# A flag's sense reversed: which of two bodies stands first in TensorE's program

## The chip, the core and the metric

The kernel runs on one core of one Trainium2 chip. The metric is the device time of one execution in microseconds (us). Five engines work side by side, each on its own instruction stream: TensorE (PE in the profile; its weight loads are PEld), VectorE (DVE), ScalarE (ACT), GpSimd (POOL) and SyncE (SP). They meet only through semaphores.

## The reference

Two transformer-like blocks on x of 8 sequences x 512 tokens x 128 features. Layer 0 adds a state-space branch and then a feed-forward branch; layer 1 adds a gated linear attention and a feed-forward of LoRA experts. What matters here is the feed-forward of layer 0:

```
_tlin(x, w, s) = einsum('bsi,oi->bso', x, w) * s
h = silu(_tlin(x, w1_w, w1_s)) * _tlin(x, w2_w, w2_s)
h = gelu(_tlin(h, h1_w, h1_s))
h = gelu(_tlin(h, h2_w, h2_s))
return _tlin(h, w3_w, w3_s)
```

The weights w1_w to w3_w are ternary: -1, 0 or 1, in float32.

## The kernel before

The program has two stages. `front` computes the modulations, the state-space branch and the feed-forward of layer 0 for all eight sequences; `attention_lora` computes layer 1. Each stage is one block in which every engine has a hand-written stream, and ends with two barriers of all engines, one at the block's end (shown at L445 for the first stage) and one behind the clearing of the semaphores (L148).

Activations of the feed-forward are split into two rounded parts, high and low (`h_hi`, `h_lo`, `ffn_g_hi`, `ffn_g_lo`), so that two fast products of type float32r with rounded weights `w_hi` give the result of float32. This is right only if the weights are exact in the rounded type. ACT sums the low halves of all weights (L819, `w_junk`), PE adds the four sums (L1063), DVE turns the result into a flag of one number (L641, `w_inexact`), and PE reads the flag into a register (L1172) and branches (L1173). If it is set, PE runs `run(False, ...)`, whose products take the raw weights as plain float32; if not, `run(True, ...)`, whose products take `w_hi` as float32r. With the reference's ternary weights the flag is 0 and `run(True, ...)` runs. Both bodies do the same work in the same order: the transposition of the first normalised sequence (`flip_ffn`, whose instructions have L243), the first tiles (L1113 for the high part, L1117 for the low part), then four pairs of sequences with 24 tiles each (L1072, L1073), and in the end the transposition of the last two results (`flip_y`, again L243). They signal the same semaphores as often, so the other engines' streams don't know which one ran.

In the program of PE the `If` body comes first and the `Else` body behind it. The `If` body ends with a jump over the `Else` body to the stage's end; the `Else` body is followed by the stage's end. PE's part ahead of the branch is `prepare`.

Around the branch the other engines do this. DVE: flag (L641), moments of sequence 0 (`moments_ffn`: L483, L487, L492), modulations (L526), moments of `z` of sequence 1, `apply_ffn(0)` which writes `h_full` (L513), `centre(1)` (L563), `update_centred(1)` (L571), `moments_ffn(1)`, `low_h(0)` which writes `h_lo` (L586), `apply_ffn(1)` (L513). GpSimd: the reciprocal roots (L713) and the addition of a bias to x (L726). ACT: `bring_ffn(0)`, which writes `h_hi` and then `ffn_h` from the transposition (L249). At the stage's end ACT scales the last result (`bring_y`, L836), PE transposes it, and DVE adds it to x (L590).

Of the kernel before, what the change touches and what calls it, by code (L numbers as in the profile page):

```python
# [18 lines left out]
I32 = mybir.dt.int32  # L19
I16 = mybir.dt.int16  # L20
ACT = mybir.ActivationFunctionType
ALU = mybir.AluOpType
# [48 lines left out]
def build(nc, d, out):  # L71

    with ExitStack() as ctx:
        def sb(name, shape, dt=F32):
            return ctx.enter_context(nc.sbuf_tensor(name, shape, dt))

        r = {"set_up": ctx.enter_context(nc.semaphore("set_up"))}

        r["x"] = sb("x", [P, B, T, D])
        r["cols"] = sb("cols", [P, COLS])  # L80
        r["ident"] = r["cols"][:, C_IDENT:C_IDENT + P]
        r["neg_half"] = sb("neg_half", [P, T])
        r["mod"] = sb("mod", [P, 2, 4, B])
        r["gain_ffn0"] = sb("gain_ffn0", [P, B])
        r["l1"] = sb("l1", [P, L1COLS])
        r["wo"] = r["l1"][:, L_WO:L_WO + 2 * D].rearrange("p (q n) -> p q n", q=2)
        r["ar1"] = r["l1"][:, L_AR1:L_AR1 + AR]
        r["war2"] = r["l1"][:, L_WAR2:L_BG].rearrange("p (k n) -> p k n", k=KH)
        r["low_rows"] = r["l1"][:, L_LOW:L_LOW + 1]
        r["gate_bias"] = sb("gate_bias", [P, 1])  # L90
        r["eye8"] = sb("eye8", [P, NH])
        r["ones"] = sb("ones", [P, P])


        with ExitStack() as layer0:
            def sb0(name, shape):
                return layer0.enter_context(nc.sbuf_tensor(name, shape, F32))

            r["gain_attn0"], r["bias_attn0"] = sb0("gain_attn0", [P, B, D]), sb0("bias_attn0", [P, B, D])
            r["ssm_u"] = sb0("ssm_u", [2 * SD, S])  # L100
            for name, shape in (("out", [P, T, D]), ("hT", [P, S]), ("state", [P, S]), ("zn", [P, T, D])):
                r[f"ssm_{name}"] = [sb0(f"ssm_{name}{s}", shape) for s in range(2)]

        r["v_hi"] = sb("v_hi", [P, VCOLS], F32R)
        r["v_lo"] = sb("v_lo", [P, VCOLS], F32R)
        r["m_hi"] = sb("m_hi", [P, NH, P], F32R)
        r["m_lo"] = sb("m_lo", [P, NH, P], F32R)
        r["sel"] = sb("sel", [P, NH, P], F32R)
        r["sel32"] = sb("sel32", [P, 2, P], F32R)
        r["b1s"] = sb("b1s", [3 * GLO, HID], F32R)  # L110
        r["b2s"] = sb("b2s", [3 * GLO, D], F32R)
        r["gain_attn1"] = sb("gain_attn1", [P, B, D])
        r["gain_ffn1"] = sb("gain_ffn1", [P, B, D])
        r["h_split"] = [[sb(f"h_{q}{s}", [P, S], F32R) for q in ("hi", "lo")] for s in range(2)]
        r["h_full"] = [sb(f"h_full{s}", [P, S]) for s in range(2)]
        r["norm_out"] = [sb(f"norm_out{s}", [P, S]) for s in range(2)]
        psum = [ctx.enter_context(nc.psum_tensor(f"bank{n}", [P, S], F32)) for n in range(8)]

        with ExitStack() as block0:
            def sb0(name, shape, dt=F32):  # L120
                return block0.enter_context(nc.sbuf_tensor(name, shape, dt))

            r["w_hi"] = sb0("w_hi", [P, WCOLS], F32R)
            r["w_raw"] = sb0("w_raw", [P, WCOLS])
            r["w_inexact"] = sb0("w_inexact", [1, 1], I32)
            r["w_scale"] = r["cols"][:, C_SCALE:C_SCALE + 4 * KH].rearrange("p (k m) -> p k m", k=4)
            r["wp"] = r["cols"][:, C_WP:C_WP + SD]
            front(nc, d, r, psum)
        attention_lora(nc, r, psum, out)
# [123 lines left out]
def front(nc, d, r, psum):  # L253
# [17 lines left out]
    with ExitStack() as ctx:  # L271
# [62 lines left out]
        w_high, w_summed, w_flagged = sem("w_high"), sem("w_summed"), sem("w_flagged")  # L334
# [70 lines left out]
        def full_at(*use):  # L405

            return AT[use] + 1

        def bank(*use):
            return psum[HOME[use]]  # L410
# [34 lines left out]
        with nc.Block() as block:  # L445
# [32 lines left out]
            def _(dve):  # L478
# [15 lines left out]
                def moments_in(b):  # L494
                    dve.wait_ge(loaded_x[b if b < SLOTS else 1 + b // 2], 16)
                    moments(n_in, b, lambda t: x_of(b)[:, t, :])

                def moments_out(b):
                    dve.wait_ge(mm, full_at("z", b))
                    moments(n_out, b, lambda t: bank("z", b)[:, t * P:(t + 1) * P])  # L500
# [9 lines left out]
                def apply(n, b, dst):  # L510
                    dve.wait_ge(n["rstd_ready"], b + 1)
                    for t in range(T):
                        ins = dve.tensor_scalar(dst[:, t, :], x_of(b)[:, t, :], n["mv"][:, b, t, 0:1], n["rstd"][:, b, t:t + 1], ALU.subtract, ALU.mult)  # L513
                    ins.then_inc(n["ready"], 1)
# [6 lines left out]
                def modulations(k0, k1, ps):  # L521

                    src = ps[:, 0:(k1 - k0) * B].rearrange("p (k b) -> p k b", b=B)
                    dst = r["mod"][:, :, :, :].rearrange("p l k b -> p (l k) b")
                    for one in range(2):
                        dve.tensor_scalar(dst[:, k0 + one:k1:2, :], src[:, one:k1 - k0:2, :], float(one), None, ALU.add).then_inc(mod_ready, 1)  # L526
# [14 lines left out]
                def gates_soon():  # L541
                    gates(0, 1, bank("mod", 0), 2)
                    ga0 = gate_col[:, 0:B]
                    dve.wait_ge(loaded_cols, 16)
                    dve.tensor_scalar(spread_col[:, 0, :], ga0, r["cols"][:, C_GAMMA:C_GAMMA + 1], None, ALU.mult)
                    dve.tensor_scalar(spread_col[:, 1, :], ga0, r["cols"][:, C_BETA:C_BETA + 1], None, ALU.mult).then_inc(mod_ready, 1)
# [66 lines left out]
                def prepare():  # L613
                    for b in slots:
                        moments_in(b)
                    apply(n_in, 0, ssm_out[0])
                    dve.wait_ge(mm, full_at("mod", 0))
                    modulations(0, 2, bank("mod", 0))
                    dve.wait_ge(loaded_cols, 16)
                    dve.wait_ge(mod_ready, 2)  # L620
                    dve.tensor_scalar(sa_bo[:, :], r["mod"][:, 0, 0, :], r["cols"][:, C_BO:C_BO + 1], None, ALU.add).then_inc(mod_ready, 1)
                    apply(n_in, 1, ssm_out[1])
                    gates_soon()
                    dve.wait_ge(loaded_rows, 16)
                    dve.wait_ge(mm, full_at("gap", 0))
                    dve.tensor_tensor(b_gap[:, :], rows[:, R_BP:R_BP + 1], bank("gap", 0)[0:STRIPS, 0:1], ALU.subtract).then_inc(gap_ready, 1)
                    dve.wait_ge(gap_ready, 1)
                    dve.tensor_tensor(b_bias[:, :], b_gap[:, :], rows[:, R_B:R_B + 1], ALU.mult).then_inc(bias_ready, 1)
                    dve.wait_ge(cleared, 3)
                    for s in slots:  # L630
                        at = slice(s * SD, (s + 1) * SD)
                        dve.tensor_copy(cw[at, s, :], bank("cw", 0)[at, 0:D]).then_inc(cw_ready, 1)
                    moments_in(2)
                    dve.wait_ge(lam_ready, 1)
                    scan(0)
                    moments_in(3)
                    moments_out(0)
                    centre(0)
                    update_centred(0)
                    dve.wait_ge(mm, full_at("flag", 0))  # L640
                    dve.tensor_scalar(r["w_inexact"][:, :], bank("flag", 0)[0:1, 0:1], 0.0, None, ALU.is_gt).then_inc(w_flagged, 1)  # L641
                    moments_ffn(0)
                    dve.wait_ge(mm, full_at("mod", 1))
                    modulations(2, 8, bank("mod", 1))
                    moments_out(1)
                    apply_ffn(0)
                    centre(1)
                    update_centred(1)
                    moments_ffn(1)
                    low_h(0)  # L650
                    apply_ffn(1)
# [310 lines left out]
            def _(pe):  # L962
# [206 lines left out]
                claim = Claims()  # L1169
                prepare(claim)  # L1170
                at = claim.made
                inexact = pe.value_load(r["w_inexact"][0:1, 0:1], min_val=0, max_val=1)  # L1172
                with pe.If(inexact):  # L1173
                    run(False, Claims(at))
                with pe.Else():
                    run(True, Claims(at))


def attention_lora(nc, r, psum, out_ap):
# [931 lines left out]
```

## Time and profile before

| | us |
|---|---|
| timed runs, median of 3 | 579.3 |
| timed runs, lowest and highest | 578.2, 579.88 |
| the profiled execution | 577.59 |
| its span, first to last instruction | 575.7 |

The page gives for each engine its busy time, and the granted clock of PE in 40 slices. A group of instructions or a timeline row has start and duration, the line of the kernel, what is written from what, and in brackets the idle time of the engine before it with what ended it. Instructions that only the sequencer runs (a branch, a drain, a wait) are not counted as busy; they show in the view of one line's instructions, marked with a q.

### The profile page before, as it was taken

The numbers are of one execution on the slowest core, as the hardware profiler recorded it, in microseconds if no ns is written. First come the engines' busy times: TensorE is split into PE (matmuls) and PEld (weight loads), VectorE is DVE, ScalarE is ACT, GpSimd is POOL, SyncE is SP. The second block draws the span as 40 slices with busy tenths as digits, with TensorE's granted clock in tenths as the row PEclk, the third lists the DMA queues.
The fourth block names the chain that finished last, engine by engine and source line by source line (L and its number), as shares of the span: only waits on it lengthen the run. The fifth ranks groups of instructions, "written<-read, shape, count | busy, mean of one in ns | idle before, by whom it ended". The sixth has DMA issues, their size and how long they took to land. (4 is left out here: it accounts for less than half of the span.)

```text
span 575.7 us, 10224 instructions
## 1 busy us (share of the span) xinstructions
PE 533.4 (93%) x3768; PEld 440.3 (76%) x3768; DVE 389.8 (68%) x1013; ACT 346.4 (60%) x627; POOL 196.8 (34%) x261
## 2 busy tenths in 40 slices
PE   7599989998999999899999999999999769999993
PEld 6558866876787688688888888888888668888873
DVE  6986968686778766467777685858596646544422
ACT  4888768767776788375555555555555324455540
POOL 3402430241021021034273645455455523344211
PEclk9789999999999999999999999999999979999998
DMA  8400000000014000000000000000000000000101
GB/s 298 150 2 1 1 0 1 1 2 0 1 36 142 2 0 2 0 1 2 1 1 2 1 1 1 1 4 1 1 1 2 1 0 1 20 19 19 37 20 38
DMA packets 10804, 11.72 MB, mean 20 GB/s; under 512 B 736, under 2 KB 9376, under 8 KB 10624
## 3 DMA queue, kind: packets, MB, share of 16 engines
q1 hardware_dynamic: 9696, 10.50, 5.5%
q8 instruction: 33, 0.54, 0.4%
q10 hardware_dynamic: 1056, 0.52, 0.3%
q14 instruction: 19, 0.16, 0.1%
HBM read 8.92 MB, written 2.10 MB: 19 GB/s over the span
## 5 line engine op out<-in xcount | busy, mean ns | idle before, releaser
L1072 PE MATMUL bank<-ffn_g_hi,w_hi 128*128 128x512 f32 x288 | 116.8, 406 | 0.1
L1073 PE MATMUL bank<-ffn_g_lo,w_hi 128*128 128x512 f32 x288 | 114.0, 396 | 0.0
L1414 DVE TENSOR_TENSOR_SCAN att_decay<-bank,norm_out 128x512 f32<-128x512 f32 x64 | 77.6, 1214 | 34.0 <-PE bank L1870 34.0
L611 DVE TENSOR_TENSOR ffn_g_lo<-ffn_full,ffn_g_hi 128x512 fp32r<-128x512 f32 x96 | 67.1, 699 | 27.3 <-ACT ffn_full L857 25.8
L1878 PEld LDWEIGHTS bank<-att_qT,h_full 128*128 128x128 f32 x512 | 66.9, 193 | 5.3 <-issue 1.6
L1878 PE MATMUL bank<-att_qT,h_full 128*128 128x128 f32 x512 | 68.8, 278 | 0.2 <-DVE att_outer L1446 0.2
L1072 PEld LDWEIGHTS bank<-ffn_g_hi,w_hi 128*128 128x128 f32 x288 | 54.3, 188 | 13.9 <-issue 1.7
L1728 ACT COPY att_qT<-bank 128x512 f32<-128x512 f32 x64 | 37.4, 587 | 44.5 <-PE bank L169 41.1
L1073 PEld LDWEIGHTS bank<-ffn_g_lo,w_hi 128*128 128x128 f32 x288 | 54.3, 189 | 11.7
L1422 DVE TENSOR_TENSOR att_prob<-bank,att_decay 128x512 f32<-128x512 f32 x64 | 42.8, 669 | 20.7 <-issue 16.4
L857 ACT ACTIVATE ffn_full<-bank,cols 128x512 f32<-128x512 f32 x64 | 44.3, 697 | 19.6 <-PE bank L1073 14.5
L1572 POOL TENSOR_TENSOR att_vw<-att_v,att_decay 128x128 f32<-128x128 f32 x64 | 26.1, 408 | 70.5 <-DVE att_decay L1414 70.5
L713 POOL TENSOR_TENSOR ssm_out_rstd<-ssm_out_var,neg_half 128x4 f32<-128x4 f32 x8 | 9.2, 1153 | 85.2 <-DVE ssm_out_var L492 85.2
L1958 PE MATMUL bank<-l,att_qT 128*128 128x155 f32 x256 | 35.6, 296 | 0.0
L1958 PEld LDWEIGHTS bank<-l,att_qT 128*128 128x128 f32 x256 | 34.2, 189 | 0.0
L1552 POOL TENSOR_TENSOR h_lo<-h_full,h_hi 128x512 fp32r<-128x512 f32 x14 | 17.9, 1278 | 44.8 <-ACT h_hi L249 44.7
L598 DVE SCALAR_TENSOR_TENSOR ffn_full<-bank,cols,norm_out 128x512 f32<-128x512 f32 x32 | 23.4, 742 | 12.8 <-ACT norm_out L843 12.7
L1072 PE MATMUL bank<-h_hi,w_hi 128*128 128x512 f32 x60 | 25.8, 431 | 5.6 <-ACT norm_out L843 2.8
L167 PE MATMUL bank<-h_hi,v_hi 128*128 128x512 f32 x56 | 25.8, 460 | 5.0 <-DVE att_state L1438 2.5
L855 ACT ACTIVATE ffn_g_hi<-bank,cols 128x512 fp32r<-128x512 f32 x32 | 22.5, 704 | 10.4 <-PE bank L1073 10.1
L167 PE MATMUL bank<-h_hi,m_hi 128*128 128x512 f32 x64 | 27.5, 429 | 0.0
L1870 PE MATMUL bank<-att_cut_in,sel 128*128 128x512 f32 x64 | 26.9, 440 | 0.1
(226 smaller groups left out, 1222.4 us busy)
## 6 DMA issues: line engine op xcount, KB each, us to landing
out<-att_vw SPq DMA_DIRECT2D x8, 256.0 KB, 2.3
x<-in_x SPq DMA_DIRECT2D x3, 512.0 KB, 12.2
w_raw<-in_w_all SPq DMA_DIRECT2D x1, 1152.0 KB, 8.7
w_raw<-in_w_all SPq DMA_DIRECT2D x1, 768.0 KB, 9.9
stage<-in_sel SPq DMA_DIRECT2D x1, 640.0 KB, 7.7
v_raw<-in_v_all SPq DMA_DIRECT2D x1, 576.0 KB, 5.9
x<-in_x ACTq DMA_DIRECT2D x2, 256.0 KB, 3.5
w_raw<-in_w_all SPq DMA_DIRECT2D x1, 512.0 KB, 5.1
```

Of the source, the lines that this page charges most:

```text
L167: pe.matmul(acc, w[0], x[0], start=start, stop=False)
L611: dve.tensor_tensor(lo, full[j % 4][:, :], hi.bitcast(F32), ALU.subtract).then_inc(low, 1)
L857: act.activation(full[j % 4][:, :], ps, ACT.Gelu, scale=scale).then_inc(gelu_ready, 1)
L1072: pe.matmul(acc, w[0], x[0], start=start, stop=False)
L1073: return pe.matmul(acc, w[0], x[1], start=False, stop=stop)
L1414: dve.tensor_tensor_scan(decay[at % ND][:, :], bank("decay", b, k)[:, :], ident4[:, :], 0.0, ALU.mult, ALU.add).then_inc(decay_ready, 1)
L1422: dve.tensor_tensor(prob[k][:, :], bank("score", b, k)[:, :], decay[at % ND][:, :], ALU.mult).then_inc(prob_ready, 1)
L1572: pool.tensor_tensor(vw[s][:, :, hs], v[s][:, :, hs], last.broadcast_to([P, T, DV]), ALU.mult).then_inc(vw_ready, 1)
L1728: act.copy(qT[b % 2][:, k, :], bank("q", b, k)[:, :]).then_inc(q_ready, 1)
L1870: pe.matmul(ps[:, :], r["sel"][:, k, :], cut_in[b % 2][:, :], start=True, stop=True).then_inc(ring_mm, 1)
L1878: mm = pe.matmul(ps[:, cc], hT[s][:, cc], qT[s][:, k, cc], start=True, stop=True)
L1958: mm = pe.matmul(ps[t // 2][:, at:at + D + AR], hid[b % 2][:, k, t * P:(t + 1) * P], r["war2"][:, k, :], start=(k == 0 and t % 2 == 0), st ...
```

## The change

The flag is computed with the opposite comparison (1 if the sum of the low halves is not above 0) and is called `w_exact`; the two bodies change places in PE's program. `run(True, ...)` is now the `If` body, which follows the branch directly and ends with the jump; `run(False, ...)` is the `Else` body.

```diff
-            r["w_inexact"] = sb0("w_inexact", [1, 1], I32)
+            r["w_exact"] = sb0("w_exact", [1, 1], I32)
...
-                    dve.tensor_scalar(r["w_inexact"][:, :], bank("flag", 0)[0:1, 0:1], 0.0, None, ALU.is_gt).then_inc(w_flagged, 1)
+                    dve.tensor_scalar(r["w_exact"][:, :], bank("flag", 0)[0:1, 0:1], 0.0, None, ALU.is_le).then_inc(w_flagged, 1)
...
-                inexact = pe.value_load(r["w_inexact"][0:1, 0:1], min_val=0, max_val=1)
-                with pe.If(inexact):
+                exact = pe.value_load(r["w_exact"][0:1, 0:1], min_val=0, max_val=1)
+                with pe.If(exact):
+                    run(True, Claims(at))
+                with pe.Else():
                     run(False, Claims(at))
-                with pe.Else():
-                    run(True, Claims(at))
```

## Rows read from the trace of the kernel before

**Rows 1.** The page: span, busy time of each engine, the instruction queue (packets, MB).
```profile
span 575.7 us, 10224 instructions
...
PE 533.4 (93%) x3768; PEld 440.3 (76%) x3768; DVE 389.8 (68%) x1013; ACT 346.4 (60%) x627; POOL 196.8 (34%) x261
...
q8 instruction: 33, 0.54, 0.4%
```

**Rows 2.** Instructions of L1172 and L1173: duration in ns, first and last start in us.
```profile
L1173 PEldq COMPARE_BRANCH  x1: 3814/3814/3814, 21.4 to 21.4; - x1
...
L1172 PEldq TENSOR_LOAD <-w_inexact x1: 483/483/483, 20.5 to 20.5; - x1
...
L1172 PEldq SEQ_ASSERT  x1: 28/28/28, 21.3 to 21.3; - x1
```

**Rows 3.** DMA queues from 21.3 to 25.2 us: packets, MB, share of 16 engines.
```profile
q8 instruction: 1, 0.02, 2.3%
```

**Rows 4.** Timeline around the branch: start and duration in us.
```profile
23.39 1.11 DVE L513 TENSOR_SCALAR h_full<-x,ffn_in_mv,ffn_in_rstd 128x128 f32<-128x128 f32 x4
...
25.34 0.71 PEld L243 LDWEIGHTS bank<-cols,h_full 128*128 128x128 f32 x4 [5.14 <-DVE h_full L513]
...
25.96 1.14 DVE L571 SCALAR_TENSOR_TENSOR x<-ssm_zn,ssm_out_rstd,x 128x128 f32<-128x128 f32 x4 [0.43 <-POOL x L726]
26.50 0.78 ACT L249 ACTIVATE h_hi<-bank,mod 128x512 fp32r<-128x512 f32 x1 [1.72 <-PE bank L243]
...
27.17 0.77 ACT L249 ACTIVATE ffn_h<-bank,mod 128x512 f32<-128x512 f32 x1
...
27.37 2.04 PE L1113 MATMUL bank<-h_hi,w_hi 128*128 128x512 f32 x4 [0.92 <-issue]
...
28.54 0.68 DVE L586 TENSOR_TENSOR h_lo<-ffn_h,h_hi 128x512 fp32r<-128x512 f32 x1
...
29.27 2.08 PE L1117 MATMUL bank<-h_lo,w_hi 128*128 128x512 f32 x4
...
30.13 1.12 DVE L513 TENSOR_SCALAR h_full<-x,ffn_in_mv,ffn_in_rstd 128x128 f32<-128x128 f32 x4 [0.91 <-POOL ffn_in_rstd L713]
```

**Rows 5.** Timeline at the end of the front stage.
```profile
240.48 0.69 ACT L836 ACTIVATE ffn_h<-bank,gain_ffn 128x512 f32<-128x512 f32 x1 [1.55 <-PE bank L1073]
...
241.22 0.66 PE L243 MATMUL bank<-cols,ffn_h 128*128 128x128 f32 x4 [0.34 <-ACT ffn_h L836]
241.91 0.69 DVE L590 TENSOR_TENSOR x<-x,bank 128x512 f32<-128x512 f32 x1 [0.31 <-PE bank L243]
...
243.87 0.29 PEld L167 LDWEIGHTS bank<-h_hi,v_hi 128*128 128x128 f32 x1 [2.24 <-issue]
```

**Rows 6.** Instructions of L445, the barrier at the end of the front stage.
```profile
L445 ACTq DRAIN  x1: 717/717/717, 240.5 to 240.5; - x1
L445 PEldq DRAIN  x1: 698/698/698, 241.2 to 241.2; - x1
L445 DVEq DRAIN  x1: 724/724/724, 241.9 to 241.9; - x1
```

**Rows 7.** Busy time and counts in two windows (PE, PEld, DVE, ACT, POOL, clock, DMA); then L1878.
```profile
25.20:241.90 216.70, 205.61 (x972) 159.59 (x972) 160.24 (x417) 160.35 (x272) 39.91 (x40) 0.99 0.04 13
243.80:252.80 9.00, 8.90 (x39) 7.71 (x40) 3.77 (x5) 8.23 (x15) 3.94 (x6) 0.84 0.00 0
...
L1878 PE MATMUL bank<-att_qT,h_full x512: 270/275/421, 253.3 to 470.7; 128*128 128x128 f32 x171
```

**Rows 8.** The same view for the three stretches of lower granted clock (third value from the end).
```profile
21.40:31.70 10.30, 5.41 (x14) 3.44 (x15) 8.75 (x43) 6.21 (x11) 4.67 (x4) 0.50 0.03 6
...
243.30:246.70 3.40, 2.80 (x10) 2.54 (x11) 1.57 (x4) 2.48 (x5) 1.00 (x4) 0.50 0.00 0
...
461.70:468.60 6.90, 3.82 (x17) 3.69 (x18) 4.98 (x12) 1.27 (x3) 1.58 (x8) 0.51 0.00 0
```

**Rows 9.** Timeline of PE after its longest rest in the attention stage.
```profile
464.78 1.09 PE L1939 MATMUL bank<-cols,att_wide 128*96 128x128 f32 x4 [7.08 <-DVE att_wide L1482]
```

## Prediction

> **What bounds the kernel now.** I read the page first [rows 1]: TensorE (PE) is busy 93% of a 575.7 us span and the next engine 68%, so the kernel is PE-bound on the whole. The change adds and removes no matmul. It moves the one place where PE's instruction stream jumps, so only two short stretches matter: the branch near 21 us, and the end of the front stage near 242 us. The view of one line's instructions gives the branch [rows 2]. The flag is read at 20.5 us by a load of 483 ns, the last instruction ahead of the branch starts at 21.3 us and takes 28 ns, and the compare-and-branch of L1173 starts at 21.4 us and takes 3814 ns, until 25.2 us. While it runs, one packet of about 16 KB moves on the queue of kind "instruction" [rows 3]. The page counts 33 such packets, 0.54 MB, over the span [rows 1]. I read this as: the jump goes to code that isn't loaded, and PE stands still until it is.
>
> The timeline around it shows who waits [rows 4]. The first PE work behind the branch, the transposition L243, starts its weight load at 25.34 us. Its input, h_full, was finished by VectorE (DVE) at 23.39 + 1.11 = 24.50 us. The profile names DVE as the releaser of 5.14 us of idle time there, but DVE had been done for 0.84 us. With under 0.1 us for a semaphore (ScalarE (ACT) ends h_hi at 26.50 + 0.78 = 27.28 and PE's next matmul starts at 27.37), the branch makes this step late by about 0.8 us and no more; the other 3 us of the jump lie under DVE's normalisation.
>
> At the end of the front [rows 5], PE's last transposition starts at 241.22 us when ACT has scaled the last y. It ends at 241.88, DVE's last addition runs 241.91 to 242.60, and then all engines meet at the barrier of L445: DVE's drain starts at 241.9 and takes 724 ns, PE's starts at 241.2 and takes 698 ns [rows 6]. So DVE arrives last, at 242.65, and PE 0.7 us before it. A second barrier (L148) follows and PE begins the attention stage at 243.87. Nothing is taken across these barriers: whatever delays the last engine to arrive delays everything behind it by as much.
>
> **The change, part by part.** (a) Reversed test. DVE's comparison of one element (L641) is is_le instead of is_gt on the same operand. Same form, cost 0.
>
> (b) The branch now falls through. What that costs no row of PE shows. Bounds: above, what the jump costs now, 3.8 us [rows 2]; below, a few hundredths, as the 28 ns of the sequencer's own instruction just before it [rows 2]. I take the lower end, since the code that follows is in the program's order and all other crossings of code in the trace go by without a stop. PE is then ready at about 21.5 us, waits for h_full, and starts L243 at 24.55 instead of 25.34: 0.8 us earlier.
>
> Does that pass on? ACT had waited 1.72 us for PE, so h_hi would start at 25.7 and end at 26.5, and the four L1113 matmuls run 26.55 to about 28.4 instead of 27.37 to 29.2 (they start 0.43 us apart at this clock) [rows 4]. But next come the L1117 matmuls, which want h_lo of DVE L586. That instruction runs 28.54 to 29.22, and it stands behind DVE's moments of the other sequence (L483, L487, L492), which wait for the update L571 (25.96 to 27.10), which itself waited 0.43 us for GpSimd's addition of L726 [rows 4]. None of these waits for L243. ffn_h, the input that does, is ready at 27.94 already now and 0.6 us ahead of DVE. So L1117 starts at 29.27 as before, and the 0.8 us turn into idle time before it. The next transposition, at 31.30, waits for DVE's second h_full (30.13 + 1.12 = 31.25), again DVE's and GpSimd's chain. I take 0 as the gain, and 0.8 as its other end.
>
> (c) A jump at the end of the stage. The body for exact weights now stands ahead of the other one, and must leap over it to reach the barrier. How far? It runs 972 matmuls and 972 weight loads [rows 7]; by the code 704 of its products use rounded weights. In the other body these are plain float32, and the trace has such a product as two instructions of each kind (L1878: 256 in the code, 512 in the trace [rows 7]). So the body to be leapt over has about 1944 + 2 x 704 = 3350 instructions, the same that is leapt over now. The price is then that of today's jump: 3.8 us [rows 2]. For bounds: its one packet took 2.3% of 16 engines over 3.9 us = 1.43 us [rows 3], the mean of all 33 is 0.4% x 16 x 575.7 / 33 = 1.1 us [rows 1]. So 3.5 us is the low end; with another packet as slow, 4.1 the high one.
>
> When does it start? PE's sequencer might run ahead of the last transposition's wait. But the drains show it in order: PE's starts at 241.2, just when the waiting transposition starts; ACT's at 240.5 when its last activation starts after a wait of 1.55 us; DVE's at 241.9 likewise [rows 5, 6]. I take it that the jump too starts at 241.22 and ends at 241.22 + 3.81 = 245.03. With 0.1 us until the next instruction (25.2 to 25.34 at the start [rows 2, 4]), PE reaches the barrier at about 245.1 instead of being there 0.7 us early. The barrier opens 245.1 - 242.65 = 2.45 us later. From the low and high price: 2.1 to 2.8.
>
> At this place a rule speaks against the sum. The Trainium skill's page "Advanced Engine Details and Errata", section "Control Flow Timing", gives some 51 ns for an unconditional branch and some 108 ns for compare-and-branch. By it (c) would be hidden in the 1.4 us that PE's sequencer has to spare, and the total would be 0. The row has 3814 ns for a compare-and-branch, so the rule holds, if at all, for targets that are loaded. The Trainium skill's page "Runtime: NRT & Kernel Launch", section "Instruction fetch mechanics", says that a taken branch whose target lies outside the loaded window has to wait for a DMA of it; the trace agrees, with the one packet.
>
> (d) The clock behind the barrier. PE's granted clock is at the half level (1.2 of 2.4 GHz) in 243.3 to 246.7, 2.8 us beyond PE's restart [rows 5, 8]. PE is busy 8.90 of the 9.00 us from 243.8 to 252.8 [rows 7], so time at half clock counts there. PE now rests 2.0 us; it will rest 4.5 us. The nearest row of a longer rest is the one of 7.08 us: work resumes at 464.78 and the full clock is back at 468.6, 3.8 us later [rows 8, 9]. The stretch at the start is the other: 25.4 to 31.7, 6.3 us, but with gaps in the work [rows 4, 8]. Half of each us more is lost: (3.8 - 2.8)/2 = 0.5 us taken; bounds 0 and (6.3 - 2.8)/2 = 1.75.
>
> Sum: 0 + 0 + 2.45 + 0.5 = +2.95 us, bounds -0.8 + 2.1 + 0 = 1.3 and 0 + 2.8 + 1.75 = 4.55. Queues of other engines are not touched: no DMA, and no instruction of ACT, DVE, GpSimd or SyncE, is moved. The profiled run took 577.6 us, its span 575.7; with the change 580.5 and 578.7. That execution lies 1.7 us below the median of the timed runs (579.3), so for the median I expect 579.3 + 2.95 = 582.2.
>
> **The rivals.** 1) The last jump is hidden: the sequencer takes it ahead of PE's waits, or its target is fetched ahead. For it: PE's sequencer has nothing else to do there, and PE waits 0.34 us for ACT before the last transposition [rows 5]. Against it: the drains' order. It decides if the jump is over by 242.6. Then 0 to -0.8: 579.3 to 578.5. Chance 0.13.
> 2) The gain at the start comes through, as PE's five microseconds of idle time there suggest. For it: PE is the bound of the span. Against it: L586 and L513 on DVE. -0.8 + 2.45 + 0.5 = +2.15: 581.5. Chance 0.08.
> 3) Faster. The jump hidden as in 1, and the earlier start brings PE's full clock back sooner than 31.7 us: in 27.4 to 31.7 PE works at half clock, and had it only the 2.8 us of the other restart, (6.3 - 2.8)/2 = 1.75 us would be saved, if DVE follows. -0.8 - 1.75 = -2.55: 576.8. It decides only when the jump costs under 1.4 us. Chance 0.02.
> 4) Something further behind the jump, such as a second stop for the next piece of code (another 2 to 3 us): 585. Chance 0.03.
> 5) The change doesn't do what it says (the jump now taken stays where it is): 579.3. The diff leaves little room; 0.01.
> My forecast, the sum as worked out, has 0.73.
>
> **How the numbers follow.** A difference of 0.3%, 1.7 us, is about what measurement can tell here. Slower by more: forecast 0.73 less 0.02 for its lowest corner, with rivals 2 and 4: 0.82. Faster by more: rival 3, 0.02. The same: 0.16. The likeliest case with its bounds spans 580.6 to 583.9. The three runs before scatter by 0.8 us around their median, so I close at 580.5 and 584.3; rivals 1, 3, 5 and most of 4 stay outside, just under 0.2.
>
> **What would show it.** After the change: no long compare-and-branch at L1173; an instruction-queue packet and an unconditional branch of 3.5 to 4 us at about 241 us; PE's first weight load of the front's transposition at 24.55 us; L1117 unchanged at 29.3 us; PE last at the barrier; the attention stage's first weight load near 246.3 us; half clock until about 250 us. It is wrong if that first load is still near 243.9 us (rival 1), or if everything from 29 us on is 0.8 us early (rival 2).

## The result, and the profile after

| | before | after |
|---|---|---|
| timed runs, median (8 of each) | 578.75 us | 581.28 us |
| lowest to highest | 577.42 to 579.89 | 580.68 to 582.96 |
| ratio | 1 | 1.0047, 95% interval 1.003 to 1.0063 |
| the profiled execution, and its span | 577.59, 575.7 | 581.13, 579.2 |

The changed kernel is 2.5 us slower. Run once more, beside 23 other runs of the kernel before, it was slower by 3.2 us (below). The profile shows the jump in its new place. The view of one line's instructions, for L1173 and for the barrier L445 of the changed kernel (durations in ns, first and last start in us):

```profile
L1173 PEldq COMPARE_BRANCH  x2: 78/1680/3283, 21.4 to 241.3; - x2
...
L445 DVEq DRAIN  x1: 726/726/726, 242.0 to 242.0; - x1
L445 PEldq DRAIN  x1: 60/60/60, 244.7 to 244.7; - x1
...
L445 ACTq EVENT_SEMAPHORE  x1: 17/17/17, 244.9 to 244.9; - x1
```

The branch at 21.4 us now takes 78 ns instead of 3814 [rows 2]. An unconditional jump, which the profile also names COMPARE_BRANCH, starts at 241.3 us and takes 3283 ns. DVE is done at 242.0 + 0.73 = 242.75, but PE's drain starts only at 244.7, so PE is the last to arrive, and the other engines pass the barrier at 244.9. One 16 KB packet of code moves meanwhile, as it did at the start before [rows 3]; the DMA view from 241.3 to 244.6 us:

```profile
DMA packets 1, 0.02 MB, mean 5 GB/s; under 512 B 0, under 2 KB 0, under 8 KB 0
...
q8 instruction: 1, 0.02, 1.8%
```

Now the start, as a timeline of the changed kernel, to be held against [rows 4]:

```profile
24.48 1.12 PE L243 MATMUL bank<-cols,h_full 128*128 128x128 f32 x4 [4.24 <-DVE h_full L513]
...
25.64 0.78 ACT L249 ACTIVATE h_hi<-bank,mod 128x512 fp32r<-128x512 f32 x1 [0.93 <-PE bank L243]
...
26.51 2.04 PE L1113 MATMUL bank<-h_hi,w_hi 128*128 128x512 f32 x4 [0.92 <-issue]
...
28.46 0.68 DVE L586 TENSOR_TENSOR h_lo<-ffn_h,h_hi 128x512 fp32r<-128x512 f32 x1
...
29.20 2.08 PE L1117 MATMUL bank<-h_lo,w_hi 128*128 128x512 f32 x4 [0.65 <-DVE h_lo L586]
30.06 1.12 DVE L513 TENSOR_SCALAR h_full<-x,ffn_in_mv,ffn_in_rstd 128x128 f32<-128x128 f32 x4 [0.91 <-POOL ffn_in_rstd L713]
```

L243 and L1113 are 0.9 us earlier. L1117 is not: it starts at 29.20 instead of 29.27, and has a new wait of 0.65 us for DVE's h_lo. All of this profile's early part lies 0.07 us earlier, DVE's h_lo too.

The end of the stage, to be held against [rows 5]:

```profile
241.31 0.66 PE L243 MATMUL bank<-cols,ffn_h 128*128 128x128 f32 x4 [0.34 <-ACT ffn_h L836]
242.01 0.69 DVE L590 TENSOR_TENSOR x<-x,bank 128x512 f32<-128x512 f32 x1 [0.31 <-PE bank L243]
245.94 1.28 ACT L1757 ACT_TABLE_LOAD   x1 [4.68 <-PEq L148]
245.95 0.19 PEld L167 LDWEIGHTS bank<-h_hi,v_hi 128*128 128x128 f32 x1 [4.22 <-issue]
```

PE's last transposition is 0.09 us later than before, PE's first weight load of the attention stage 245.95 - 243.87 = 2.08 us later. What is left of the difference comes after it. The attention stage's time on PE and its last drain, first the window and L1382 of the kernel before (243.87 us to PE's drain at 569.3), then those of the changed kernel (the columns of the windows as in [rows 7]):

```profile
243.87:569.30 325.43, 309.82 (x2668) 265.65 (x2668) 208.33 (x489) 168.85 (x327) 144.45 (x201) 0.99 0.02 7
...
L1382 PEldq DRAIN  x1: 703/703/703, 569.3 to 569.3; - x1
```

```profile
245.95:572.40 326.45, 310.87 (x2669) 266.56 (x2669) 208.20 (x489) 168.94 (x327) 144.36 (x201) 0.98 0.02 7
246.30:249.70 3.40, 3.40 (x16) 3.21 (x15) 2.31 (x4) 3.05 (x6) 1.05 (x4) 0.50 0.00 0
...
L1382 PEldq DRAIN  x1: 1158/1158/1158, 572.4 to 572.4; - x1
```

So the span's 3.5 us are 0.1 until the last transposition, 2.0 for the jump, 1.0 more in the attention stage, and 0.45 in PE's last drain. Not all of the 1.0 us lies at the barriers. The row behind PE's longest rest [rows 9] divides it; in the changed kernel it is

```profile
467.11 1.09 PE L1939 MATMUL bank<-cols,att_wide 128*96 128x128 f32 x4 [7.08 <-DVE att_wide L1482]
```

From PE's first weight load of the stage to this row it is 467.11 - 245.95 = 221.16 us, and 464.78 - 243.87 = 220.91 in the kernel before. So the longer stretch of half clock behind the barriers, in which PE works 3.4 us (246.3 to 249.7) instead of 2.8, costs 0.25 us more. The other 0.8 us of the stage, and the 0.45 of the drain, come later. PE's clock was half at the end of this profile and full at the end of the kernel before's; a window around the last drain, in the kernel before and then in the changed kernel (columns as in [rows 7], the clock third from the end):

```profile
568.80:570.80 2.00, 0.66 (x4) 0.52 (x4) 0.76 (x2) 0.46 (x1) 0.00 (x0) 1.00 0.00 0
```

```profile
570.80:573.40 2.60, 1.93 (x8) 1.40 (x7) 0.00 (x0) 0.58 (x1) 0.00 (x0) 0.50 0.00 0
```

That isn't tied to the change. Over all 13 profiles of this study the last drain takes 0.70 us where the clock is still full (the kernel before and two later kernels, one of each order of the bodies) and 1.16 us where it is half (the ten others, a kernel with no jump at the end among them).

### The profile page after: what moved, and what is told of

Read it like the earlier page. It is cut to its first block and busy times, and to the rows that moved or that the text cites. A ratio compares the mean times of both kernels' runs of the same rounds, so it can differ in the third digit from the quotient of the medians.

```text
span 579.2 us, 10225 instructions
## 1 busy us (share of the span) xinstructions
PE 536.0 (93%) x3768; PEld 442.5 (76%) x3768; DVE 389.6 (67%) x1013; ACT 346.4 (60%) x627; POOL 196.7 (34%) x261
## 5 line engine op out<-in xcount | busy, mean ns | idle before, releaser
L1878 PEld LDWEIGHTS bank<-att_qT,h_full 128*128 128x128 f32 x512 | 66.9, 193 | 5.3 <-issue 1.6
L1878 PE MATMUL bank<-att_qT,h_full 128*128 128x128 f32 x512 | 68.8, 278 | 0.2 <-DVE att_outer L1446 0.2
L855 ACT ACTIVATE ffn_g_hi<-bank,cols 128x512 fp32r<-128x512 f32 x32 | 22.5, 704 | 10.4 <-PE bank L1073 10.0
```

What stands on the lines that cost most here:

```text
L1878: mm = pe.matmul(ps[:, cc], hT[s][:, cc], qT[s][:, k, cc], start=True, stop=True)
```

## The experiments

Each experiment is compared with runs of the kernel before that were taken beside it on the same chip. For the first three here, and for the hint at the start further down, these are 35 runs (median 579.19, 577.21 to 580.22 us).

**No jump at the end.** The body for inexact weights is left out of the program.

```diff
                 with pe.If(exact):
                     run(True, Claims(at))
-                with pe.Else():
-                    run(False, Claims(at))
```

> The changed kernel without its Else body: the products with raw float32 weights are left out of the program, so no jump stands at the end of the stage. With the reference's weights the same instructions run as in the changed kernel. My theory (the whole difference is the jump at the end; what the fall-through gives at the start is absorbed by DVE): L243 starts near 24.5 us as in the changed kernel, L1117 at 29.2, the attention stage's first weight load at 243.8 to 244.0, and the time is that of the kernel before, within 0.5 us. Rival 'the gain at the start comes through': 0.8 us faster than before. Rival 'the program's layout or the fall-through itself costs something': slower than before by 0.5 us or more.

Measured: 579.01 us, ratio 0.9999 (0.9985 to 1.0013). The timeline shows the whole early start of L243 and the same L1117, and PE on time at the second stage:

```profile
24.41 1.12 PE L243 MATMUL bank<-cols,h_full 128*128 128x128 f32 x4 [4.24 <-DVE h_full L513]
...
29.14 1.22 PE L1117 MATMUL bank<-h_lo,w_hi 128*128 128x512 f32 x2 [0.65 <-DVE h_lo L586]
...
243.81 0.19 PEld L167 LDWEIGHTS bank<-h_hi,v_hi 128*128 128x128 f32 x1 [2.24 <-issue]
```

The fall-through brings nothing that can be measured, and the loss of the changed kernel goes with the jump. A gain of 0.8 us (0.14%) lies just inside the interval, so this time alone doesn't rule it out; the unmoved L1117 does.

**The jump hinted.** A prefetch hint for the jump, at the start of the fourth pair, in the changed kernel; the two bodies are named by hand so that the jump can carry it.

```diff
+                        if mark and i == PAIRS - 1:
+                            mark.append(pe.mark_branch_hint_location())
...
-                with pe.If(exact):
-                    run(True, Claims(at))
-                with pe.Else():
+                pe.br_cond(exact, "w_exact_body", "w_inexact_body")
+                with nc.body("w_exact_body", valid_engines=[pe.engine]):
+                    mark = [None]
+                    run(True, Claims(at), mark)
+                    pe.br("w_bodies_end").branch_hint(mark[1])
+                with nc.body("w_inexact_body", valid_engines=[pe.engine]):
                     run(False, Claims(at))
+                    pe.br("w_bodies_end")
+                nc.switch_bb("w_bodies_end")
```

> The changed kernel with a prefetch hint for the jump at the end, placed at the start of the fourth pair of sequences, some 500 instructions ahead of the jump. Nothing is left out. If the 3.28 us of the jump are the loading of code that isn't there, the hint takes them off the path: the jump takes under 0.5 us, PE reaches the barrier ahead of DVE, the attention stage starts near 243.9 and the time is that of the kernel before (plus or minus 0.5 us). Rival 'the jump waits for PE's matmuls or costs what it costs whatever is loaded': the jump stays at 3.3 us and the time 2.5 us over the kernel before.

Measured: 578.67 us, ratio 0.9995 (0.9981 to 1.0009). The jump and PE's first weight load behind the barriers:

```profile
L1179 PEldq COMPARE_BRANCH  x1: 346/346/346, 242.0 to 242.0; - x1
...
241.97 0.42 PEld L243 LDWEIGHTS bank<-cols,ffn_h 128*128 128x128 f32 x4 [0.58 <-ACT ffn_h L836]
244.62 0.19 PEld L167 LDWEIGHTS bank<-h_hi,v_hi 128*128 128x128 f32 x1 [2.24 <-issue]
```

(In this execution the last transposition comes 0.75 us later than before the change; from there to the attention stage it takes 2.65 us, as before the change.) The hint itself ran at 184.0 us and took 55 ns. One 16 KB packet of code moves between 185 and 190 us, where the changed kernel moves none, and none moves during the jump. The same jump over the same 3400 instructions takes 0.35 us if its target was asked for ahead. So the price was the loading.

**A short body to jump over.** The Else body is 16 small matmuls.

```diff
                 with pe.Else():
-                    run(False, Claims(at))
+                    warm(7, 16)
```

> The changed kernel with an Else body of 16 small matmuls in place of the products with raw float32 weights, which are left out; the jump at the end of the stage stays, but over 65 instructions instead of 3400. If the price is the loading of code, the jump takes about 0.1 us (the fall-through took 78 ns) and the time is that of the kernel before, within 0.5 us. If a taken jump costs by itself, it stays near 3.3 us and the time near 2.5 us over the kernel before. If the target happens to lie past the end of what is loaded, it costs part of 3.3 us.

Measured: 579.44 us, ratio 0.9996 (0.998 to 1.0011). The fall-through took 73 ns and the jump 180 ns:

```profile
L1173 PEldq COMPARE_BRANCH  x2: 73/126/180, 22.2 to 241.9; - x2
```

No packet of code moves during this jump (241.9 to 242.2 us).

**A middling body to jump over.** The same with `warm(7, 200)`, 800 instructions. Beside it, and beside the next experiments but the hint at the start, there are 23 other runs of the kernel before (median 579.64, 577.4 to 580.73).

> As the run with the short Else body, but with 200 small matmuls (800 instructions) in its place; the products with raw float32 weights are left out. If the price is one loading of code that isn't there, whatever the distance, the jump takes 3.3 us again as over 3400 instructions, and the time is that of the changed kernel (2.1 to 2.5 us over the kernel before). If the price grows with the distance, about 0.9 us, and it hides under DVE's last addition.

Measured: 582.76 us, ratio 1.006 (1.004 to 1.008), the loss of the changed kernel in full. The longer of the two is the jump:

```profile
L1173 PEldq COMPARE_BRANCH  x2: 78/1726/3374, 21.4 to 241.6; - x2
```

Over 65 instructions 0.18 us, over 800 as much as over 3400. The price is one loading and not a matter of distance.

**The first jump hinted, in the kernel before.** The order of the bodies is that of the kernel before; the branch at the start carries a hint from the top of PE's program.

```diff
+                mark = pe.mark_branch_hint_location()
                 prepare(claim)
...
-                with pe.If(inexact):
+                pe.br_cond(inexact, "w_inexact_body", "w_exact_body").branch_hint(mark)
```

> The kernel before (exact body last, jumped to at 21.4 us) with a prefetch hint for that jump at the start of PE's program. Nothing is left out. If the hint works, the jump takes under 0.5 us instead of 3.81, L243 starts at 24.5 instead of 25.34. My theory says the time then doesn't change (within 0.5 us of the kernel before), since L1117 waits for DVE's h_lo at 29.2 whatever PE did; the rival 'the start is on the path' says 0.8 us faster.

Measured: 579.06 us, ratio 1.0001 (0.9987 to 1.0016). The branch takes 386 ns instead of 3814. This profile lies 1.6 us later than that of the changed kernel from the branch on, since its flag came later, but PE's wait for h_full is 4.25 us, as in the changed kernel, so PE was ready in time:

```profile
L1174 PEldq COMPARE_BRANCH  x1: 386/386/386, 23.1 to 23.1; - x1
...
26.11 1.12 PE L243 MATMUL bank<-cols,h_full 128*128 128x128 f32 x4 [4.25 <-DVE h_full L513]
...
30.84 2.08 PE L1117 MATMUL bank<-h_lo,w_hi 128*128 128x512 f32 x4 [0.65 <-DVE h_lo L586]
```

With the jump of the start made cheap where it stands, the time doesn't move either. L1117 has the same 0.65 us of waiting. That settles the start.

Why the flag came later is in the clock: PE worked at half of it from 8.2 to 15.0 us here, and at full clock in the same window of the kernel before:

```profile
8.20:15.00 6.80, 6.21 (x20) 3.07 (x19) 4.89 (x26) 3.14 (x4) 1.21 (x2) 0.50 1.02 404
```

```profile
8.20:15.00 6.80, 5.64 (x34) 3.43 (x33) 6.20 (x30) 4.43 (x8) 1.37 (x2) 1.00 1.01 390
```

Of the 13 profiles, seven have no such stretch and their branch starts at 21.3 to 21.8 us; four have one of 3.4 us, with the branch at 22.2 to 22.5; two have one of 6.8 us, with the branch at 23.1 and 23.2. Both orders of the bodies occur in each of the three groups.

**The changed kernel once more.**

> The changed kernel itself once more, for a difference from as many runs as the others have. The jump moves PE's first weight load of the attention stage by 2.08 us in the profile; eight runs differed by 2.53 us at their medians, and against the larger set of runs of the kernel before by 2.1. If the jump is all, the difference is 2.1 plus or minus 0.3. If PE's clock behind the longer rest costs the 0.5 us that I had put down for it, 2.6.

Measured: 582.87 us against 579.64, ratio 1.0055 (1.0036 to 1.0074), 3.2 us. The interval of the ratio holds both 2.1 and 3.2 us, so it doesn't tell the two expectations (2.1 and 2.6) apart. The profile shows why 2.1 isn't a fixed number: here the jump took 3879 ns, and the half clock lasted from 245.0 to 251.9, of which PE, back at 247.49, worked 4.4 us.

```profile
L1173 PEldq COMPARE_BRANCH  x2: 78/1978/3879, 22.5 to 242.2; - x2
...
245.00:251.90 6.90, 4.41 (x17) 4.06 (x18) 3.15 (x5) 3.60 (x7) 2.08 (x5) 0.51 0.01 2
...
469.03 1.09 PE L1939 MATMUL bank<-cols,att_wide 128*96 128x128 f32 x4 [7.08 <-DVE att_wide L1482]
```

The attention stage's first weight load is at 247.46 us, 5.23 us behind the last transposition's (2.65 in the kernel before), so the jump's delay is 2.6 us here. From that load to PE's longest rest it takes 221.57 us, 0.66 more than in the kernel before.

**PE's array kept at work during the jump.** Twelve matmuls that nobody reads, ahead of the jump, in the changed kernel.

```diff
                     run(True, Claims(at))
+                    for _ in range(12):
+                        pe.matmul(psum[7][:, :], r["w_hi"][:, 0:P], r["w_hi"][:, 0:S], start=True, stop=True)
```

> The changed kernel with 12 added matmuls of 512 columns that nobody reads, ahead of the jump, so that PE's array works for 2.6 us while its sequencer waits for code. The jump is unchanged (3.3 us, ends near 244.7). In the profile of the changed kernel PE rests 4.0 us and then works 3.4 us at half clock. If that rest costs clock, the attention stage now starts at the full clock and the time is 1.5 us below the changed kernel, about 1 over the kernel before. If the clock is no part of the difference, the time stays at that of the changed kernel (2.1 to 2.5 over the kernel before). If the jump waits until the added matmuls are done, it gets later and the time grows by up to 2.6 us.

Measured: 580.33 us, ratio 1.0014 (1.0 to 1.0029), 2.5 us less than the changed kernel on the same chip, where 1.5 had been expected. The jump was a slow one, 3850 ns, from 242.0; the added matmuls ran beside it and the attention stage began at full clock:

```profile
242.35 3.00 PE L1176 MATMUL bank<-w_hi 128*128 128x512 f32 x12
247.27 0.47 PE L167 MATMUL bank<-h_hi,v_hi 128*128 128x512 f32 x1 [1.92 <-PEq L148]
...
247.20:250.60 3.40, 3.33 (x20) 3.05 (x21) 2.11 (x4) 3.02 (x6) 1.00 (x5) 1.00 0.00 0
...
466.84 1.09 PE L1941 MATMUL bank<-cols,att_wide 128*96 128x128 f32 x4 [7.07 <-DVE att_wide L1484]
...
247.25:572.00 324.75, 309.16 (x2668) 264.99 (x2668) 208.14 (x489) 168.13 (x327) 144.25 (x201) 0.99 0.02 7
```

From the stage's first weight load (247.24 us) to PE's longest rest it takes 219.60 us here, against 221.16 and 221.57 in the two profiles of the changed kernel and 220.91 in the kernel before. (The whole stage takes 324.75 us, with half clock at its end as in the changed kernel.) The clock term is real: the work behind the barriers costs 1.3 to 2.0 us more when it starts with a stretch of half clock. It isn't a constant of either kernel, though. The kernel before had the half clock behind the barriers in its profile [rows 8]; the one without the Else body and the two with a hinted jump had the same rest of 2.0 us and kept the full clock.

**The clock's share taken away.** The hinted kernel with three such matmuls behind the last transposition, so that PE rests 1.33 us at the barriers instead of 2.0.

```diff
                     run(True, Claims(at), mark)
+                    for _ in range(3):
+                        pe.matmul(psum[7][:, :], r["w_hi"][:, 0:P], r["w_hi"][:, 0:S], start=True, stop=True)
```

> The changed kernel with the hint for the jump and three added matmuls of 512 columns behind PE's last transposition, which nobody reads. They fill 0.65 us of PE's rest of 2.0 us at the barriers and end about when DVE arrives. The runs of the kernel before fall in two clusters, near 577.4 and 579.7 us. If these are executions with and without a stretch of half clock behind the barriers, the rest of 1.35 us leaves the clock up more often: median about 577.8, 1.2 us faster than before. If the clusters come from elsewhere: 579.0, as the run with the hint alone.

Measured: 578.27 us against 579.64, ratio 0.9983 (0.9972 to 0.9993), all twelve runs between 577.62 and 579.14. It ran again beside 29 other runs of the kernel before (median 579.6, 577.32 to 580.28), which also serve the two experiments below:

> The kernel with hint and three added matmuls once more, on the same chip as the two others, to compare them with. Expected 0.15 to 0.25% faster than the kernel before, as the first time.

Measured: 578.09 us, ratio 0.999 (0.9973 to 1.0007): the same direction, but not beyond its interval.

**The three matmuls in the kernel before.** They stand behind `run(True, ...)` in its Else body.

> The kernel before with the three added matmuls behind PE's last transposition and nothing else. If the 1.4 us by which hint and added matmuls beat the kernel before come from the clock behind the barriers, they come here too: about 578.3 against 579.6, with PE at full clock when the attention stage starts. If the fall-through at the start has a part in them, this kernel stays at or near the time of the kernel before.

Measured: 577.14 us, ratio 0.9973 (0.9958 to 0.9988), the fastest kernel of the study and below the 578.3 expected. (The medians fall in different clusters of runs; the ratio, 0.27% or 1.6 us, is the better measure of the gain.) PE's end of stage and restart:

```profile
242.44 0.94 PE L1178 MATMUL bank<-w_hi 128*128 128x512 f32 x3
244.72 0.47 PE L167 MATMUL bank<-h_hi,v_hi 128*128 128x512 f32 x1 [1.33 <-PEq L148]
...
243.00:250.00 7.00, 5.67 (x31) 4.65 (x30) 4.19 (x6) 4.97 (x10) 2.65 (x5) 1.00 0.00 0
```

So the gain of the hinted and filled kernel owes nothing to the order of the bodies. The runs still fall in two clusters (576.6 to 577.3 and 578.4 to 578.8), so the clock behind the barriers isn't the clusters' only cause. They go with the granted clock as a whole. Its mean over a run was 0.975 to 0.978 in the seven runs up to 577.3 us and 0.972 to 0.975 in the five from 578.4 on; of the 29 runs of the kernel before, the eight up to 577.8 us had 0.978 and the fifteen from 579.6 on 0.969 or 0.972. The profiles show two other places where executions differ, the stretch ahead of the branch (0.9 or 1.7 us) and the one at the program's end (some 1.2 us). Why a stretch comes in one execution and not in the next stays open.

**What absorbed the start, taken away.** The hinted and filled kernel with DVE's h_lo ahead of the moments of sequence 1.

```diff
+                    low_h(0)
                     moments_ffn(1)
-                    low_h(0)
                     apply_ffn(1)
```

> The kernel with the hint and three added matmuls, and DVE's order at the start changed: h_lo of sequence 0 (L586) ahead of the moments of sequence 1. That takes away what absorbed the fall-through's gain: L1117 should start near 27.8 us instead of 29.2. DVE's second h_full gets 0.6 to 0.7 us later (31.8 instead of 31.2), for its moments now start after ffn_h at 27.1. If DVE's chain to the second h_full sets the pace there, the time is the same or up to 0.7 us longer than with the hint and the added matmuls alone (578.3); if L1117 does, 0.5 to 1 us shorter.

Measured: 578.21 us, ratio 0.9989 (0.9974 to 1.0004); 578.09 without the reordering, beside the same runs. This profile lies 1.7 us later from the start (L243 at 26.20 instead of 24.48); less that, L1117 starts at 28.35 instead of 29.20, and DVE's second h_full ends at 31.45 instead of 31.18:

```profile
26.20 1.12 PE L243 MATMUL bank<-cols,h_full 128*128 128x128 f32 x4 [4.24 <-DVE h_full L513]
...
30.07 1.91 PE L1117 MATMUL bank<-h_lo,w_hi 128*128 128x512 f32 x4
...
32.05 1.12 DVE L513 TENSOR_SCALAR h_full<-x,ffn_in_mv,ffn_in_rstd 128x128 f32<-128x128 f32 x4 [1.13 <-POOL ffn_in_rstd L713]
```

L1117 no longer waits for DVE and comes 0.85 us earlier, and still no time is won. Both moves are smaller than expected (27.8 and 31.8 us). DVE's and GpSimd's chain to the second h_full holds the pace there, as the expectation's first branch had it.

## Why the prediction was right, point by point

- *The branch falls through for a few hundredths; 0.8 us earlier at L243.* 78 ns and 0.86 us.
- *The start gains nothing.* Right, and for the reason given: L586 didn't move, L1117 got a wait of 0.65 us. The kernels with no jump at all and with the start's jump hinted differ from the kernel before by 0.01%, with intervals of some 0.15% each way. By their times alone a gain of 0.8 us (0.14%) would be at the edge of that; with L1117 unmoved in all these profiles, rival 2 is out.
- *The jump at the end starts when the last transposition starts and costs what the other cost, 3.8 us (3.5 to 4.1); the barrier opens 2.45 us later.* Order and place were right: it starts at 241.3, with the transposition at 241.31. The four profiles that have such a jump there show 3.28, 3.37, 3.85 and 3.88 us, so the low bound of 3.5 us was too high. The size isn't one of the place: the jump at the start took 3.81 us in the kernel before, and 3.37 in the same kernel with three matmuls added. From the last transposition's weight load to the attention stage's first one these four profiles take 4.64 to 5.30 us, against 2.65, so the delay was 2.0 to 2.65 us where 2.45 (2.1 to 2.8) was forecast. I had shortened the jump by the packet's own time alone, from 1.43 to the mean of 1.1 us. With 1.8% of 16 engines over 3.3 us the packet took 0.95 us here, less than that mean.
- *Rival 1, the jump hidden.* Didn't happen, but the two ways in which it can were made: by the hint, and by a target already loaded. Both gave the time of the kernel before.
- *Rivals 3 and 4.* Rival 3 wanted the full clock back sooner than 31.7 us by the earlier start. In the changed kernel's two profiles it came back at 34.6 and 33.4 us, not sooner, and little of that reaches the end: from L1117 to the last transposition they take 212.11 and 211.93 us, against 211.95. Rival 4's second stop isn't there: PE's drain ends 0.1 us behind the jump and its work resumes at 245.95, 1.2 us later, as it did before behind DVE's drain (242.65 to 243.87).
- *The clock, +0.5 us (0 to 1.75).* In the profiles the step is 0.25 and 0.66 us, up to PE's longest rest; the remainder of the 1.0 us lies at the program's end. From the timed runs it can be estimated. The added matmuls took 0.41% off the changed kernel (1.0055 to 1.0014) and 0.27% off the kernel before. The difference of 0.14%, 0.8 us, is what the clock adds to the change, though the intervals of these ratios leave more than 1 us each way. So the size held as far as can be told. The step had one thing wrong: it took the kernel before to lose its clock at the barriers each time, and three profiles with the same rest show that it need not. Where it does not, a longer rest adds the whole cost of its half-clock stretch, 1.5 to 2.0 us, and not the difference of two stretches.
- *The sum, +2.95 us.* Measured 2.5 and 3.2. With the clock kept up in both orders the ratios are 1.0014 and 0.9973; their quotient, 0.41% or 2.4 us, is an estimate of the jump alone (from runs on two chips, each against the kernel before on its own), for which 2.45 was forecast. That the sum lies between the two measured values is partly luck, since the jump's delay alone changes by 0.65 us from execution to execution.

A rule stood against the sum, the Trainium skill's 51 and 108 ns ("Advanced Engine Details and Errata", section "Control Flow Timing"). For a branch that isn't taken the runs show 73 to 81 ns and for a jump to loaded code 180 ns (346 and 386 with a hint), the same order of size or a few times more; for a target that isn't loaded they show 3.3 to 3.9 us, thirty times the larger figure or more.

## What to carry to other kernels

A branch has to be costed where it stands: a jump to code that isn't loaded stops one engine for 3.3 to 3.9 us, and what that costs is what its cover doesn't hide. Here the jump sat under DVE's work at the start, where it was free, and the change moved it in front of a barrier, where nothing hid it; moving a stall needs a look at both ends. If a jump must stand in an open place, a prefetch hint well ahead brings it to 0.35 or 0.39 us (here 58 us ahead for the jump at the end, and from the top of PE's program for the branch at the start). How near the hint may stand was not tried.

## What the runs showed of the hardware that I had not expected

- The price of a far jump scatters by 0.6 us between executions (3.28 to 3.88 us over 3400 instructions) and doesn't grow with the distance: it is 3.37 us over 800 instructions, and 0.18 us over 65, where the target is loaded. One code packet accounts for about 0.95 us of it in the changed kernel; what the rest is spent on isn't shown.
- PE's array goes on with queued matmuls while its sequencer waits for code: twelve matmuls ran from 242.35 to 245.35 us beside a jump from 242.0 to 245.9.
- A rest of 2.0 us at the barriers sometimes costs PE's full clock (the profiles of the kernel before and of the one with the short Else body) and sometimes not (three others). From the stage's first weight load to PE's longest rest it takes 220.9 to 221.6 us in the five profiles with half clock there, jumps at the end included, and 219.6 to 219.7 in the eight without. With the rest filled up to 1.33 us the clock was full in all four profiles, and the kernel before got 0.27% faster by three matmuls that compute nothing.
- Stretches of half clock come and go between executions at places that no edit touched. Ahead of the branch there was none, one of 3.4 us or one of 6.8 us, and the branch came at 21.3 to 21.8, 22.2 to 22.5 or 23.1 to 23.2 us. PE's last drain took 0.70 us at full clock and 1.16 at half. Differences of 1 us between two profiles can be this alone.
